# Last stage of a decoder kernel moved into the block of its cross-attention, with two orders changed beside it

## What is computed

```python
# second layer, cut
x = layernorm(x + mixer(x, in_proj_w, conv_w, ..., out_proj_w))           # a state-space mixer
x = layernorm(x + cross_attention(x, ctx, Wq, Wk, Wv, Wo, q_norm, k_norm)) # 32 query heads, 8 key/value heads
x = layernorm(x + ffn(x, gate, kernel, bias, lora_A, lora_B, lora_A_shared, lora_B_shared))

def ffn(x, gate, kernel, bias, lora_A, lora_B, lora_A_shared, lora_B_shared):
    base_out = x @ kernel + bias
    A_eff = einsum('bn,nri->bri', gate, lora_A)      # 16 adapters of rank 32, mixed by the gate of each batch
    B_eff = einsum('bn,nor->bor', gate, lora_B)
    Ax = einsum('bri,bti->btr', A_eff, x)
    delta = einsum('bor,btr->bto', B_eff, Ax)
    Ax_s = einsum('ri,bti->btr', lora_A_shared, x)
    delta += einsum('or,btr->bto', lora_B_shared, Ax_s)
    return base_out + delta
```

## Time and profile before

| | us |
|---|---|
| time, median of 3 runs (lowest, highest) | 2675.28 (2673.12, 2677.63) |
| the profiled execution, its own time | 2670.47 |
| its span from first to last instruction | 2668.7 |
| mixer's last output loop to the attention's start | 1642 to 1719 |
| attention, 64 steps | 1719 to 2583 |
| from there to the first matmul of the last stage | 2583 to 2598 |
| adapters, then eight batches of the last stage | 2598 to 2614 to 2669 |

### The profile page before, as it was taken

One profiled execution on the slowest core, in us unless ns is written; L12 is line 12 of the kernel. 1 busy time (PEld: TensorE's weight loads), 2 busy tenths in 40 slices (PEclk: granted clock), 3 DMA queues, 4 the chain that ended last, 5 costly groups with the idle time before them and its releaser, 6 DMA issues. The chain is left out here.

```text
span 2668.7 us, 39228 instructions
## 1 busy us (share of the span) xinstructions
PE 2508.4 (94%) x14088; PEld 2054.7 (77%) x14088; DVE 1866.1 (70%) x2540; ACT 1121.5 (42%) x2649; POOL 1059.2 (40%) x877
## 2 busy tenths in 40 slices
PE   7877699999999999999999998799999999999968
PEld 4445488888888888888888886688888888888856
DVE  4865597795886968869778595466666666666653
ACT  2321334333343343434434333355555655655531
POOL 3101265555555655556555554442322322222100
PEclk9988799999999999999999999899999999999989
DMA  4000241230421303314123141010100101100010
GB/s 151 1 0 9 103 150 48 87 115 28 142 87 60 138 32 115 115 41 149 40 90 113 47 144 60 20 37 17 41 17 25 33 18 32 33 17 17 1 55 32
DMA packets 61555, 163.83 MB, mean 61 GB/s; under 512 B 8336, under 2 KB 8976, under 8 KB 52944
## 3 DMA queue, kind: packets, MB, share of 16 engines
q1 hardware_dynamic: 59232, 158.14, 17.4%
q10 hardware_dynamic: 2160, 3.43, 0.4%
HBM read 158.92 MB, written 2.62 MB: 61 GB/s over the span
## 5 line engine op out<-in xcount | busy, mean ns | idle before, releaser
L260 PE MATMUL pair<-XH,d_w_hi 128*128 128x512 f32 x1160 | 474.8, 409 | 28.3 <-POOL d_w_lo L1325 10.5
L261 PE MATMUL pair<-XL,d_w_hi 128*128 128x512 f32 x1160 | 462.4, 399 | 0.0
L262 PE MATMUL pair<-XH,d_w_lo 128*128 128x512 f32 x1160 | 461.8, 398 | 0.0
L1443 DVE TENSOR_TENSOR_SCAN d_decay<-d_decay,m_delta 128x1024 f32<-128x1024 f32 x128 | 359.6, 2810 | 13.0 <-DMA d_decay<-token_decays 11.5
L1344 POOL TENSOR_TENSOR d_decay<-d_decay,d_cb 128x1024 f32<-128x1024 f32 x128 | 309.2, 2416 | 135.3 <-DVE d_decay L1443 125.5
L1325 POOL TENSOR_TENSOR d_w_lo<-d_w,d_w_hi 128x512 fp32r<-128x512 f32 x144 | 186.9, 1301 | 283.7 <-ACT d_w_hi L1207 283.0
L260 PEld LDWEIGHTS pair<-XH,d_w_hi 128*128 128x128 f32 x1160 | 220.4, 190 | 86.7 <-issue 19.9
L1428 DVE SCALAR_TENSOR_TENSOR d_hs<-pair,d_conv,d_hs 128x1016 f32<-128x1016 f32 (+2 forms) x192 | 242.9, 1265 | 31.9 <-ACT d_hs L1232 27.4
L262 PEld LDWEIGHTS pair<-XH,d_w_lo 128*128 128x128 f32 x1160 | 220.2, 190 | 53.3
L261 PEld LDWEIGHTS pair<-XL,d_w_hi 128*128 128x128 f32 x1160 | 220.7, 190 | 47.3
L1349 POOL TENSOR_TENSOR d_gated_lo<-d_gated,d_gated_hi 128x512 fp32r<-128x512 f32 x128 | 173.3, 1356 | 154.6 <-ACT d_gated_hi L1251 154.6
(11 more groups left out here) (276 smaller groups left out, 6072.8 us busy)
## 6 DMA issues: line engine op xcount, KB each, us to landing
d_decay<-token_decays SPq DMA_DIRECT2D x64, 1024.0 KB, 4.9
d_w<-in_L_w_groups SPq DMA_DIRECT2D x144, 256.0 KB, 2.7
e_w<-in_L_w_heads SPq DMA_DIRECT2D x80, 256.0 KB, 2.7
d_wo<-in_L_wo_groups SPq DMA_DIRECT2D x64, 256.0 KB, 5.0
X<-in_x SPq DMA_DIRECT2D x8, 256.0 KB, 10.3
b_ctx<-in_ctx SPq DMA_DIRECT2D x8, 256.0 KB, 11.9
e_ctx<-in_ctx_t SPq DMA_DIRECT2D x4, 512.0 KB, 6.9
out<-X SPq DMA_DIRECT2D x8, 256.0 KB, 2.0
```

Source lines behind the costliest of these rows:

```text
L260: pe.matmul(out, wh, xh, start=first, stop=False)
L261: pe.matmul(out, wh, xl, start=False, stop=False)
L262: return pe.matmul(out, wl, xh, start=False, stop=last)
L1443: v.tensor_tensor_scan(r, r, m["DELTA"][:], 0.0, ALU.mult, ALU.add).then_inc(q["decay"], 1)
```

## The change

The order of three things changes, and the last stage moves.

1. Mixer, last group: POOL splits `e.w_lo(b - 2)` in batch b from b = 2 on, in the place where `e.w_lo(b - 1)` stood; both `ctx_lo` come behind the loop.
2. Attention: the key and value weights (items 8 and 9) are split by a function of their own, `keys_in`, in the same step as before, but on ACT ahead of `probs_hi` and on POOL ahead of the step's other weights.
3. The last stage stands inside the attention's block. Its tiles lie on areas that are free by then. SP fetches its inputs in the last head, all on one queue. MIX is built after step 58; AT, the shared A adapter, and W, the base weight, are split on ACT, DVE and POOL between the last steps; the A adapters are mixed on PE in three places between the last three batches (`adapters_a`), the B adapters behind the last `out` (`adapters_b`). The A adapters are split in two halves (AH, AL), `low(b)` is `three_pass` with 12 matmuls, in two banks by turns; the bias is added on POOL, ahead of DVE's sum. In the last steps turns(2, 3) stand ahead of turn_probs(63), and the banks of the transposes are swapped.

```diff
+ITEMS_KV = (8, 9)
...
     if kh == HK:
-        return ()
-    return [NI * kh + x for x in ((0, 1), (2, 3), (4, 5), (6, 7), (8, 9), (), (), ())[b]]
+        return []
+    return [NI * kh + x for x in ((0, 1), (2, 3), (4, 5), (6, 7), (), (), (), ())[b]]
+
+
+def keys_in(n):
+
+    kh, b = n // NB + 1, n % NB
+    return [NI * kh + x for x in ITEMS_KV] if b == 4 and kh < HK else []
...
                             gated_lo(g, b, (0,))
-                            if last_group and b <= EARLY:
-                                e.w_lo(pool, b - 1)
-                            elif last_group:
-                                e.ctx_lo(pool, 0)
+                            if last_group and 2 <= b:
+                                e.w_lo(pool, b - 2)
                             gated_lo(g, b, (1,))
...
                 group(GM - 1, True)
+                e.ctx_lo(pool, 0)
                 norm_rstd(c, pool, s, NB - 1)
                 e.ctx_lo(pool, 1)
...
+        MIX = e.place("f_mix", [P, NT, NB, RL], F32, "wo")
...
+        W = e.place("f_w", [P, KD, D], F32, "wo", GQ * D)
+        WH, WL = e.place("f_w_hi", [P, KD, D], F32R, "decay"), e.place("f_w_lo", [P, KD, D], F32R, "decay", KD * D)
+        AH = e.place("f_a_hi", [P, KD, NB, R2], F32R, "decay", 2 * KD * D)
+        AL = e.place("f_a_lo", [P, KD, NB, R2], F32R, "decay", 2 * KD * D + KD * NB * R2)
...
+                sp.wait_ge(q["q_proj"], TAIL)
+                sp.dma_start(LA[:], a["L1_ffn_la"]).then_inc(fq["la_in"], 16)
+                sp.dma_start(LB[:], a["L1_ffn_lb"]).then_inc(fq["la_in"], 16)
+                sp.wait_ge(q["out_ready"], TAIL)
+                sp.dma_start(SEL[:], a["L1_ffn_sel"]).then_inc(fq["mix_in"], 16)
+                for t in range(NT):
+                    for n in range(P // RL):
+                        row = t * (P // RL) + n
+                        sp.dma_start(GATE[n * RL:(n + 1) * RL, t, :],
+                                     a["L1_ffn_gate_t"][row:row + 1, :].broadcast_to([RL, NB])).then_inc(fq["mix_in"], 16)
+                sp.dma_start(W[:], a["L1_ffn_kernel"].rearrange("(k p) n -> p k n", p=P)).then_inc(fq["w_in"], 16)
+                sp.dma_start(AT[:], a["L1_ffn_as_t"].rearrange("(k p) r -> p k r", p=P)).then_inc(fq["w_in"], 16)
+                sp.dma_start(BIAS[:], a["L1_ffn_bias"].rearrange("(o n) -> o n", o=1).broadcast_to([P, D]))\
+                  .then_inc(fq["w_in"], 16)
+                sp.wait_ge(q["kv_proj"], U)
+                for x in range(2):
+                    sp.dma_start(BT[RL:, x, :], a["L1_ffn_bs_t"]).then_inc(fq["bt_in"], 16)
...
+                def adapters_a(k):
+                    if k == 0:
+                        pe.wait_ge(fq["la_in"], 32)
+                        pe.wait_ge(fq["mix"], NT)
+                        pe.wait_ge(q["k_lo"], U)
+                    elif k == 2:
+                        pe.wait_ge(q["exp"], GQ * U)
+                    for n in range(NT):
+                        last = pe.matmul(am_bank(k), LA[:, n, k * P:(k + 1) * P],
+                                         MIX[:, n, :, :].rearrange("p b r -> p (b r)"), start=n == 0, stop=n == NT - 1)
+                    last.then_inc(fq["am"], 1)
+
+                def adapters_b(h):
+                    if h == 0:
+                        pe.wait_ge(q["pt_lo"], 2 * U)
+                    for n in range(NT):
+                        last = pe.matmul(c.bank[4 + h][:, :], MIX[:, n, 4 * h:4 * h + 4, :].rearrange("p b r -> p (b r)"),
+                                         LB[:, n, :], start=n == 0, stop=n == NT - 1)
+                    last.then_inc(fq["bt_ready"], 1)
+
+                def low(b):
+                    t = slice(b * S, (b + 1) * S)
+                    if b == 0:
+                        pe.wait_ge(fq["am_lo"], KD)
+                        pe.wait_ge(fq["at_lo"], KD)
+                        pe.wait_ge(q["o_lo"], U)
+                    if b == 1:
+                        pe.wait_ge(q["acc"], U)
+                    if b >= 2:
+                        pe.wait_ge(fq["mid"], b - 1)
+                    pe.wait_ge(s.lo, b + 1)
+                    for k in range(KD):
+                        last = three_pass(pe, low_bank(b), AH[:, k, b, :], AL[:, k, b, :], c.XH[:, k, t], c.XL[:, k, t],
+                                          k == 0, k == KD - 1)
+                    last.then_inc(fq["low_ready"], 1)
+
+                def base(b):
+                    t = slice(b * S, (b + 1) * S)
+                    bank = c.bank[2 + b % 2]
+                    if b == 0:
+                        pe.wait_ge(fq["w_lo"], KD)
+                    if b >= 2:
+                        pe.wait_ge(fs.summed, b - 1)
+                    for k in range(KD):
+                        three_pass(pe, bank[:, :], c.XH[:, k, t], c.XL[:, k, t], WH[:, k, :], WL[:, k, :], k == 0, False)
+                    pe.wait_ge(fq["mid"], b + 1)
+                    pe.wait_ge(fq["bt"], b + 1)
+                    pe.matmul(bank[:, :], MID[:, b % 2, :], BT[:, b % 2, :], start=False, stop=True)\
+                      .then_inc(fq["out_ready"], 1)
...
                 turn_probs(U - 2)
+                adapters_a(0)
+                adapters_a(1)
                 score(U - 1)
                 pe.wait_ge(q["q_lo"], U)
-                turns(0, 1)
+                turns(0)
+                pe.wait_ge(fq["am_lo"], 2)
+                turns(1)
                 out(U - 3)
                 attend(U - 2)
+                turns(2, 3)
                 turn_probs(U - 1)
-                turns(2, 3)
+                adapters_a(2)
                 out(U - 2)
                 attend(U - 1)
+                adapters_a(3)
                 turns(4, 5)
                 out(U - 1)
+                adapters_b(0)
+                adapters_b(1)
                 turns(6, 7)
+                low(0)
+                for b in range(NB):
+                    if b + 1 < NB:
+                        low(b + 1)
+                    base(b)
...
+                def f_at_hi():
+                    act.wait_ge(fq["w_in"], 48)
+                    act.wait_ge(q["kv_proj"], U)
+                    for k in range(KD):
+                        act.activation(AH[:, k, :, RL:], AT[:, k, :].rearrange("p (o r) -> p o r", o=1)
+                                       .broadcast_to([P, NB, RL]), ACT.Copy).then_inc(fq["at_hi"], 1)
+
+                def f_w_hi(*slices):
+                    for k in slices:
+                        act.activation(WH[:, k, :], W[:, k, :], ACT.Copy).then_inc(fq["w_hi"], 1)
+
+                def am_hi(k):
+                    act.wait_ge(fq["am"], max(k + 1, 2))
+                    act.activation(AH[:, k, :, 0:RL], am_bank(k).rearrange("p (b r) -> p b r", b=NB), ACT.Copy)\
+                       .then_inc(fq["am_hi"], 1)
...
                     evac_kv(n + 3)
+                    for m in keys_in(n):
+                        e.w_hi(act, m)
                     probs_hi(n + 1)
                     exp(n + 2)
...
+                f_at_hi()
+                f_w_hi(0, 1)
                 o_hi(U - 3)
                 q_hi(U - 1)
                 probs_hi(U - 2)
+                am_hi(0)
+                am_hi(1)
                 exp(U - 1)
                 turned(0, 1)
+                f_w_hi(2, 3)
                 o_hi(U - 2)
+                turned(2, 3)
                 probs_hi(U - 1)
-                turned(2, 3)
+                am_hi(2)
                 o_hi(U - 1)
+                am_hi(3)
                 turned(4, 5)
                 turned(6, 7)
+                for b in range(NB):
+                    if b == 0:
+                        act.wait_ge(fq["bt_in"], 32)
+                    act.wait_ge(fq["bt_ready"], b // 4 + 1)
+                    if b >= 2:
+                        act.wait_ge(fq["out_ready"], b - 1)
+                    act.activation(BT[0:RL, b % 2, :], c.bank[4 + b // 4][(b % 4) * RL:(b % 4 + 1) * RL, :],
+                                   ACT.Copy).then_inc(fq["bt"], 1)
+                    act.wait_ge(fq["low_ready"], b + 1)
+                    act.activation(MID[:, b % 2, :], low_bank(b), ACT.Copy).then_inc(fq["mid"], 1)
...
                     k_power(n + 3)
-                    for m in weights_in(n):
+                    for m in keys_in(n) + weights_in(n):
                         e.w_lo(pool, m)
                     q_power(n + 3)
...
+                def bias(b):
+                    if b == 0:
+                        pool.wait_ge(fq["w_in"], 48)
+                    pool.wait_ge(s.turned, b + 1)
+                    pool.tensor_tensor(c.X[:, b, :], c.X[:, b, :], BIAS[:], ALU.add).then_inc(fq["biased"], 1)
...
+                f_w_lo(0, 1)
+                norm_rstd(c, pool, s, 5)
+                f_w_lo(2, 3)
+                norm_rstd(c, pool, s, 6)
+                norm_rstd(c, pool, s, 7)
+                for b in range(3):
+                    bias(b)
+                for b in range(NB):
```

(18 more changed lines are left out.)

195 lines of the change are left out of this document (51 added, 144 removed).

## The result

| | before | changed |
|---|---|---|
| time, median (lowest, highest), first comparison | 2675.45 us (2673.12, 2677.63) | 2600.40 us (2598.45, 2603.03) |
| ratio, 95% interval | | 0.972 (0.9703 to 0.9737) |
| the profiled execution, its span | 2668.7 | 2600.0 |

The change makes the kernel 75 us faster by the medians, 70 to 79 by the interval. So the question is which terms were too small, and why the range didn't hold them.

What follows compares the result with a forecast made beforehand. PE (94% busy) was taken as the bound, so only its waits, its work and what follows its last matmul could be won. 17.2 + 17.1 + 32.8 = 67.1 off the median 2675.28 gave 2608.2, range 2601 to 2620.

Steps and rivals of the forecast that it cites:

- Mixer: Mixer's last output loop: PE's six waits for POOL cost 17.5 with the lower clock, less 0.3 for `ctx_lo(0)`: 17.2 gained.
- Heads: Attention's seven changes of head: PE's waits for the low key and value weights go, 2 x 3.57 + 5 x 2.0 = 17.1.
- Tail: Between attention and last stage: the first low-rank product begins at 2590.8 instead of 2614.4, 23.6 gained.
- 19.6 + 7.1 + 7.1 + 3: Tail from 2554 to the first low-rank product: PE's work that stays, B mix, A mix, and remaining waits.
- 0.49 for 0.8, 1.32 for 2.0, none for 0.3: Tail waits forecast: 0.8 left ahead of score(63), 2.0 where turns(2, 3) wait for banks, 0.3 ahead of attend(63).
- Last stage: Eight batches at 4.94 instead of 5.95, and 0.7 from the bias leaving DVE's path at the end; 9.2 gained.
- the tie between 64 and 128 columns: Last stage's low-rank matmuls: forecast took 0.062 each (64-column weights); rival at 0.12 (128-column) gave 2614, chance 0.22.
- The step from the trace to the median: Whole kernel: 2603.4 summed for the profiled execution, put at 2608.2 because that execution was 4.8 below the median.
- the four terms: Forecast gains: mixer 17.2, change of head 17.1, tail 23.6, last stage 9.2; together 67.1.
- Range: Whole kernel's time, 2601 to 2620: below, no tail waits, better small matmuls, run spread; above, two rivals together.

## Why the prediction was off, point by point

- **Mixer, right.** 35.9 measured, 35.8 forecast; all 17.4 of the waits and their clock came back, and `ctx_lo(0)` cost nothing that shows. The stretch to the first turn gained 2 more than the term: 1.4 ahead of batch 1, behind a wait of 4.7 that both have, which is chance (see above), and 0.4 behind the loop. Luck is in the 35.8 against 53.3 too: in two other traces with the old order the same six batches took 54.6 and 54.7. With the mixer's order alone the stretch gained 17.7.
- **Heads, right.** In the trace of before the seven changes of head cost 2.0 and, in two, 3.57, as worked out. With the mixer's order alone all seven cost 2.0, with the last stage alone one cost 3.57, so how many fall to the lower clock is chance. The first three steps took 0.9 longer in the changed kernel's trace and 2.9 in its two others.
- **Tail, mechanism right, size off: the term of the sum that failed.** "19.6 + 7.1 + 7.1 + 3" gives 36.8, measured 34.1. The waits were 1.8 and not 3: 0.49 for 0.8, 1.32 for 2.0, none for 0.3. The mixes took 13.7 and not 14.2. And the 19.6 of PE's work that "stays" was wrong by 1.0: without the waits the same instructions needed 18.6. About half of this is the clock. The mean of 0.95 hides that it was 1.00 up to 2578 and low only behind the last wait, where four transposes took 1.09 for the 0.60 of the four before:

```profile
2576.90 0.60 PE L240 MATMUL pair<-ident,X 128*128 128x128 f32 x4
2580.31 1.09 PE L240 MATMUL pair<-ident,X 128*128 128x128 f32 x4 [2.81 <-DVE X L230]
```

  The other half is the end of the last matmul ahead of each wait, which counts as busy (0.39 for a matmul of 512 columns) where its successor would otherwise start after 0.23. Besides, the trace used was 1.5 to 1.8 short in this stretch, so the usual gain is nearer 28 than 26.3.
- **Last stage, right mechanism, 1.1 too little.** The small matmul cost 0.060 for 0.062, and the tie between 64 and 128 columns was decided by the right row. `low` took 0.77 and not 0.88, since the 0.14 that I had added for switching is some 0.05 there, and the base product behind it 2.95 instead of 3.00.
- **The step from the trace to the median failed, and it took the result out of the range.** In "it was 4.8 below the median of the runs" I took a difference between one execution and a median of three for a constant. The changed kernel's profiled execution lay 1.3 above its median. And the 4.8 itself was large: three later sets of nine executions of the kernel before gave 2672.29, 2672.42 and 2672.54, only some 1.9 above the trace (whether the first median is chance or owed to another chip is not on record). With 1.9 in place of 4.8 the forecast is 2605.3, and with the 4.8 that the four terms were short together 2600.5; the changed kernel's medians are 2600.40, 2601.63 and 2600.84. That the first one fell 0.6 outside the range, and the second inside, is chance; that the forecast was some 5 too high in its terms is not.
- **Range.** The lower end was 7.2 below the forecast: 3.0 for waits in the tail, and what was left for better small matmuls and the spread of the runs. The same program came to its first changed instruction at 1638.4 to 1647.0. By that scatter I estimate that a median of three carries 2 or 3, a difference of two medians more. With 2 more for each side the lower end would have been near 2597.

## What to carry to other kernels

Price a stretch whose waits go away by its work at full clock from one start to the next, not by its busy time in the old trace: ahead of each wait the last matmul's end counts as busy, and behind a long one some of the busy time is the lower clock; both go with the wait (1.0 of 19.6 here). Sum in traces, and don't carry one execution's distance from a median of three over to another kernel. Where the critical engine loses its waits, use a fill (work that must be done anyway and depends on little) cut to the length of each wait; moving a whole one only moves the wait. Compare two traces stretch by stretch along one engine's instructions, since single stretches without a wait repeat to 0.1 us where whole executions of this kernel differ by 8.

## What the runs showed of the hardware

- A matmul of 128 moving columns whose weights change every time starts every 0.060 us with weights of 64 columns and every 0.112 with 128, as the weight loads beside it do.
- The clock's way back behind a wait differs from execution to execution. Behind a wait of 3.51, the same in 12 traces, the same work took 13.48 to 13.50 in ten of them and 14.45 and 14.58 in two; those two had also had the longest waits (5.31 and 4.87) before it. Nothing later takes such a difference back: the traces' distances at 330 us are still there at 1642.
- An instruction of 0.55 us on DVE that took 1.50 beside POOL's, in four of eight batches, cost the kernel nothing: such a hold-up is worth a change only where DVE is waited for.
